# State and probability products of a linear-attention chunk as one piece over sixteen heads, with the query decayed in place

## What is computed

```python
def step(S, inp):
    qb, kb, vb = inp
    inter = jnp.einsum('bhcd,bhde->bhce', qb * decay_q[None, :, :, None], S)
    scores = jnp.einsum('bhcd,bhed->bhce', qb, kb) * dmask[None]
    intra = jnp.einsum('bhce,bhed->bhcd', scores, vb)
    S_new = lam_c[None, :, None, None] * S + jnp.einsum('bhcd,bhce->bhde', kb * decay_k[None, :, :, None], vb)
    return (S_new, inter + intra)
```

## Time and profile before

| | |
|---|---|
| median of three runs | 1953.87 us |
| the profiled execution | 1956.51 us |
| its span | 1954.7 us |
| TensorE busy | 1876.6 us (96%) |
| VectorE busy | 1084.2 us (55%) |
| ScalarE busy | 842.1 us (43%) |
| GpSimd busy | 438.3 us (22%) |
| mean granted clock of TensorE | 0.99 |
| block 0 (first q/k projection to that of block 1) | 17.05 to 122.84 us |
| end of attention (router product of block 7) | 1212.2 us |
| moved by DMA | 456.84 MB |

### The profile page before, as it was taken

How to read it: one execution, slowest core, us unless ns; L and a number is a source line. 1 busy time by engine, 2 the same in 40 slices (tenths; PEclk the granted TensorE clock), 3 DMA queues, 4 the chain that set the end, 5 groups by cost and what they waited for, 6 DMA issues and landing times.

```text
span 1954.7 us, 27560 instructions
## 1 busy us (share of the span) xinstructions
PE 1876.6 (96%) x9880; PEld 1529.3 (78%) x9880; DVE 1084.2 (55%) x2590; ACT 842.1 (43%) x1718; POOL 438.3 (22%) x438
## 2 busy tenths in 40 slices
PE   7789999999999998999999999999999999999997
PEld 5566777777777776777777778778999999999875
DVE  4556665454564563464454454353666667666566
ACT  4433443333343233334244233112666666666554
POOL 2301001001001000100100100120355666655322
PEclk9899999999999999999999999999999999999999
DMA  8988557656466447537647456687788989998597
GB/s 309 371 275 301 204 204 275 222 172 231 162 234 238 167 166 258 202 119 261 207 179 253 175 175 237 236 332 258 215 250 261 280 260 262 268 266 249 135 280 198
DMA packets 140869, 456.84 MB, mean 234 GB/s; under 512 B 17200, under 2 KB 17344, under 8 KB 123968
## 3 DMA queue, kind: packets, MB, share of 16 engines
q1 hardware_dynamic: 90720, 251.70, 36.7%
q0 software_dynamic: 49584, 203.33, 33.8%
q10 hardware_dynamic: 432, 0.07, 0.0%
HBM read 332.99 MB, written 122.04 MB: 233 GB/s over the span
## 4 chain that ended last, share of the span: by engine, by line
PE 88%; DVE 5%; DMA 3%; ACT 2%; issue 1%; another core or an unknown queue 0%; SPq 0%; POOL 0%; ACTq 0%; DVEq 0%
PE banks L797 24%; PE banks L799 24%; PE banks L798 24%; PE banks L866 5%; PE banks L880 2%; PE banks L886 2%; PE banks L992 2%; DMA att_w_lo<-att_w_split 1%; PE banks L873 1%; PE banks L830 1%; PE banks L998 1%; DMA out<-x 1%; PE banks L860 1%; DVE fin_stats L1538 0%; PE banks L908 0%
## 5 line engine op out<-in xcount | busy, mean ns | idle before, releaser
L797 PE MATMUL banks<-xT_hi,ffn_gate_up_hi_lo 128*128 128x512 f32 x704 | 288.5, 410 | 9.7 <-DMA xT_lo<-xt_scratch 3.2
L799 PE MATMUL banks<-xT_hi,ffn_gate_up_hi_lo 128*128 128x512 f32 x704 | 276.3, 392 | 0.0
L798 PE MATMUL banks<-xT_lo,ffn_gate_up_hi_lo 128*128 128x512 f32 x704 | 275.4, 391 | 0.0
L1070 ACT COPY q_one_head<-qT 32x128 f32<-32x128 f32 x512 | 150.9, 295 | 121.9 <-PE banks L866 116.8
L797 PE MATMUL banks<-moe_gu_hi,moe_xT_hi 128*128 128x352 f32 x568 | 189.4, 333 | 0.0
L799 PE MATMUL banks<-moe_gu_hi,moe_xT_lo 128*128 128x352 f32 x568 | 183.3, 323 | 0.0
L798 PE MATMUL banks<-moe_gu_lo,moe_xT_hi 128*128 128x352 f32 x568 | 182.6, 321 | 0.0
L797 PEld LDWEIGHTS banks<-xT_hi,ffn_gate_up_hi_lo 128*128 128x128 f32 x704 | 132.9, 189 | 44.3 <-issue 7.0
L683 POOL DMA_INDIRECT ffn_out<-moe_y,moe_x x71 | 124.9, 1760 | 155.4 <-ACT moe_gu_hi L1131 59.8
L798 PEld LDWEIGHTS banks<-xT_lo,ffn_gate_up_hi_lo 128*128 128x128 f32 x704 | 133.0, 189 | 29.2 <-issue 3.6
L799 PEld LDWEIGHTS banks<-xT_hi,ffn_gate_up_hi_lo 128*128 128x128 f32 x704 | 132.5, 188 | 28.8
(11 more groups left out here) (318 smaller groups left out, 4139.8 us busy)
## 6 DMA issues: line engine op xcount, KB each, us to landing
ffn_gate_up_hi_lo<-ffn_gate_up_split SPq DMA_DIRECT2D x66, 1024.0 KB
ffn_down_hi_lo<-ffn_down_split SPq DMA_DIRECT2D x66, 512.0 KB, 4.4
att_w_hi<-att_w_split SPq DMA_DIRECT2D x112, 256.0 KB, 5.3
att_w_lo<-att_w_split SPq DMA_DIRECT2D x112, 256.0 KB, 5.8
x_normed_by_expert<-x_normed POOLq DMA_DIRECT2D x26, 771.0 KB, 15.9
ffn_w_raw<-w_ffn SPq DMA_DIRECT2D x44, 384.0 KB, 6.0
ffn_gate_up_split<-ffn_gate_up_hi_lo SPq DMA_DIRECT2D x11, 1024.0 KB, 4.9
x_in<-x SPq DMA_DIRECT2D x32, 256.0 KB, 5.2
```

What stands on the lines that cost most here:

```text
L797: pe.matmul(out_ap, l_hi, r_hi, start=start, stop=False)
L798: pe.matmul(out_ap, l_hi, r_lo, start=False, stop=False)
L799: return pe.matmul(out_ap, l_lo, r_hi, start=False, stop=stop)
L1070: op = act.copy(qz[r, g % 2, j, :], qT[r, g, c * P:(c + 1) * P])
```

## The change

The two pieces become one, IP(c), with the state products of the four groups, then the probability products of all sixteen heads, in one bank of 512 columns. It waits for the last group's scores. `probs` has room for all four groups. ScalarE and VectorE evict the whole bank in one instruction each. The decayed q is written over q itself by a piece of its own, QD, on VectorE, which waits for ScalarE's four copies of the chunk (Z); the next block's q may be written only when the last chunk's IP is done on TensorE. All numbers of PLACES and OPENING are new. Waits for "the last weight" are now for the last of several in whichever order they stand.

```diff
+    "xin": (-31.52, -31.14, -18.03, -17.92,),
...
-    "wa": (5.53, 5.95, 9.34, 7.63, 9.92, 10.43, 10.08, 11.83, 11.97, 14.59, 17.75, 18.03, 22.85, 22.12, 24.74, 23.59,),
+    "wa": (3.51, 7.97, 8.26, 8.28, 8.94, 10.22, 10.68, 12.45, 13.8, 15.05, 16.73, 18.47, 23.22, 22.39, 22.92, 21.73,),
...
+    "QD": (21.59, 26.96, 34.86, 46,),
...
-    "ws": (3.07, 3.17, 7.17, 8.17, 10.88, 11.32, 13.32, 14.32, 15.32, 16.32, 17.32, 18.17, 23.02, 23.17, 23.32, 23.47,),
+    "ws": (16.22, 9.79, 17.24, 9.25, 19.16, 21.66, 28.21, 23.48, 32.67, 31.39, 31.98, 39.27, 40.36, 41.7, 40.49, 42.69,),
...
-    "IP": (22.6, 24.81, 28.65, 32.3, 37.22, 40.7, 46.32, 49.88,),
+    "IP": (24.98, 30.99, 40.28, 48.73,),
...
-PASSES = {"T1": 2, "QK": 12, "V": 12, "KT": 2, "S": 4, "IP": 6, "ST": 4, "OUT": 12, "T2": 2, "R1": 12, "R2": 2, "RK": 1,
+PASSES = {"T1": 2, "QK": 12, "V": 12, "KT": 2, "S": 4, "IP": 12, "ST": 4, "OUT": 12, "T2": 2, "R1": 12, "R2": 2, "RK": 1,
...
-        qd = sb("q_decayed", [G, P], scope=phase1)
-        probs = sb("probsT", [2, GH, P], scope=phase1)
+        probs = sb("probsT", [G, GH, P], scope=phase1)
...
             elif kind == "IP":
-                c, half = args
-                pe.wait_ge(v_piece, max(done("V", "S", a, c, 2 * half + 1), done("V", "V", a, c), done("V", "KT", a, c)))
-                for gl in range(2):
-                    g = 2 * half + gl
-                    pe.matmul(b[:, gl * P:(gl + 1) * P], state[:, g, :], qd[:, g, :], start=(gl == 0), stop=False,
+                c, = args
+                pe.wait_ge(v_piece, max(done("V", "S", a, c, G - 1), done("V", "V", a, c), done("V", "KT", a, c),
+                                        done("V", "QD", a, c)))
+                for g in range(G):
+                    pe.matmul(b[:, g * P:(g + 1) * P], state[:, g, :], qT[:, g, c * P:(c + 1) * P], start=(g == 0), stop=False,
                               skip_group_check=True)
-                for gl in range(2):
-                    g = 2 * half + gl
-                    cols = slice(gl * P, (gl + 1) * P)
+                for g in range(G):
+                    cols = slice(g * P, (g + 1) * P)
                     for j in range(GH):
                         r = slice(j * HD, (j + 1) * HD)
                         mm = pe.matmul(b[r, cols], v[:, c, g * P + j * HD:g * P + (j + 1) * HD],
-                                       probs[:, g % 2, j, :], start=False, stop=(gl == 1), skip_group_check=True)
+                                       probs[:, g, j, :], start=False, stop=(g == G - 1), skip_group_check=True)
...
                 if a and m == 0:
-                    act.wait_ge(p_piece, done("P", "S", a - 1, NC - 1, G - 1))
-                    act.wait_ge(v_piece, done("V", "KT", a - 1, NC - 1))
+                    act.wait_ge(p_piece, done("P", "IP", a - 1, NC - 1))
...
-                op = act.copy(oT_hi[:, 2 * half:2 * half + 2, :], chunked(b[:, 0:2 * P]))
+                op = act.copy(oT_hi[:, :, :], chunked(b))
...
-                ve.tensor_tensor(qd[:, :, :], qT[:, :, c * P:(c + 1) * P], dq[:, :, :], ALU.mult)
                 op = ve.tensor_tensor(kd[:, :], b, dk[:, :], ALU.mult)
+            elif kind == "QD":
+                c, = args
+                ve.wait_ge(a_piece, done("A", "Z", a, c, G - 1))
+                op = ve.tensor_tensor(qT[:, :, c * P:(c + 1) * P], qT[:, :, c * P:(c + 1) * P], dq[:, :, :], ALU.mult)
...
-                op = ve.tensor_tensor(oT_lo[:, gs, :], chunked(b[:, 0:2 * P]), oT_hi[:, gs, :].bitcast(F32),
-                                      ALU.subtract)
+                op = ve.tensor_tensor(oT_lo[:, :, :], chunked(b), oT_hi[:, :, :].bitcast(F32), ALU.subtract)
```

More of the change, by code:

```diff
@@ L99 @@
[L99 to L110, removed]
+    "xin": (-31.52, -31.14, -18.03, -17.92,),
+    "N1A": (-5.07,),
+    "N1B": (-1.92,),
+    "N1": (-1.67, 2.54, 2.87, 7.65,),
+    "T1": (4.49, 5.52, 7.6, 8.12,),
+    "wa": (3.51, 7.97, 8.26, 8.28, 8.94, 10.22, 10.68, 12.45, 13.8, 15.05, 16.73, 18.47, 23.22, 22.39, 22.92, 21.73,),
@@ new lines @@
+    "QK": (10.45, 10.56, 12.04, 13.66, 14.81, 14.95, 16.07, 16.43,),
+    "xr": (27.13, 32.3, 42.61, 48.08,),
+    "Z": (13.89, 15.32, 21.33, 22.5, 23.65, 23.78, 27.64, 27.9, 29.13, 29.3, 33.27, 35.14, 38.73, 42.29, 42.93, 45.06,),
+    "QD": (21.59, 26.96, 34.86, 46,),
+    "KT": (19.21, 29.28, 34.61, 46.53,),
+    "S": (17.98, 20.2, 22.22, 22.51, 25.87, 26.54, 27.95, 29.25, 32.56, 33.09, 37.34, 37.62, 43.02, 43.07, 47.64, 47.81,),
+    "V": (21.44, 22.15, 24.45, 25.52,),
+    "IP": (24.98, 30.99, 40.28, 48.73,),
@@ new lines @@
+    "ST": (27.59, 31.41, 40.69, 50.1,),
+    "OUT": (30.11, 35.5, 45.63, 50.81,),
+    "LO": (36.01, 50.91,),
+    "LN": (38.12, 53.23,),
+    "L": (38.72, 53.49,),
+    "LX": (40.86, 54.54,),
+    "x1o": (42.87, 45.14, 55.25, 60.01,),
+    "T2": (42.02, 45.02, 57.18, 57.65,),
+    "xto": (59.66,),
+    "R1": (58.72,),
+    "R2": (59.18,),
+    "SM1": (59.68,),
+    "SM2": (59.95,),
+    "SM3": (60.82,),
+    "SM4": (63.91,),
+    "CM": (61.51,),
+    "RK": (64.56,),
+    "sc": (64.43,),
+    "PG": (66.52,),
@@ L755, in sp_piece @@
                 if u < RAW:
-                    sp.wait_ge(v_piece, done("V", "W", 0, NW - 1))
+                    sp.wait_ge(v_piece, max(done("V", "W", 0, u) for u in range(NW)))
                 else:
@@ L850, in pe_attention @@
                     else:
-                        pe.wait_ge(v_piece, done("V", "W", a, 11))
+                        pe.wait_ge(v_piece, max(done("V", "W", a, 8 + k) for k in range(KT)))
                 for k in range(KT):
@@ L893, in pe_attention @@
                     else:
-                        pe.wait_ge(v_piece, done("V", "W", a, 15))
-                pe.wait_ge(v_piece, done("V", "IP", a, c, 1))
+                        pe.wait_ge(v_piece, max(done("V", "W", a, 12 + k) for k in range(KT)))
+                pe.wait_ge(v_piece, done("V", "IP", a, c))
                 for k in range(KT):
@@ L1071, in act_attention @@
             elif kind == "IP":
-                c, half = args
-                if half == 0 and c > 0:
-                    act.wait_ge(p_piece, done("P", "OUT", a, c - 1))
-                elif half == 0 and a:
-                    act.wait_ge(p_piece, done("P", "OUT", a - 1, NC - 1))
-                op = act.copy(oT_hi[:, 2 * half:2 * half + 2, :], chunked(b[:, 0:2 * P]))
+                c, = args
+                if c or a:
+                    act.wait_ge(p_piece, done("P", "OUT", *divmod(NC * a + c - 1, NC)))
+                op = act.copy(oT_hi[:, :, :], chunked(b))
             elif kind == "R1":
```

32 lines of the change are left out of this document (6 added, 26 removed), and 19 rows, old and new, of the table OPENING.

## The result

The changed kernel takes 1938.15 us (median of 4 runs, 1936.11 to 1940.40) against 1954.69 for the kernel before (1952.63 to 1955.94): ratio 0.9919, interval 0.9906 to 0.9931, so it is faster by 16.5 us. The forecast was 1939. The profiled execution took 1936.11 us, the fastest of its four, where that of the kernel before, 1956.51, lies above its whole range; so the spans, 1954.7 and 1934.3, differ by 20.4 us.

The account below looks back on a forecast made before the run. TensorE, busy 1876.6 of 1954.7 us, was taken as the bound. -9.0 + 6 - 6 - 6 = -15 us on 1956.5 gave 1941.5; the median lying 2.6 lower, the forecast was 1939 us, range 1924 to 1952.

Parts of the forecast that it names:

- Part 1: TensorE's merged piece: one step into and out of the 32-column form saved, 28 x 0.32 us behind block 0, -9.0 us.
- Part 2: Longer merged evictions and q's decay in place, on ScalarE and VectorE: covered by products of 2.8 us, cost nothing.
- Part 3: End of block 0: a split weight's store joins the transfer chain, block 1 starts at 128.6 against 122.84, +6 us.
- Part 4: Block 5: the late sixth q/k weight now goes ahead of the seventh, -6 us, ends -1.4 and -8.4.
- Part 5: TensorE's other waits behind block 0, such as k's transposes and the half product's scores: -6 us, ends -10 and +5.
- the charge of +3 for the projection of chunk 2: New wait: this projection needs the second score's bank right behind it, some 0.45 us in seven blocks, +3.
- A: Rival: block 0's chain gets no longer, TensorE let go at 120 or earlier; 1928 us, chance 0.15.
- D: Rival: no change, only the steps saved and a chain of +9 in block 0; 1953 us, chance 0.08.
- B: Rival: only the form steps are saved, the waits of parts 4 and 5 move elsewhere; 1948 us, chance 0.17.
- C: Rival: steps belong to each group of column tiles, so nothing of part 1 comes; near 1948 us, chance 0.05.
- E: Rival: slower, block 0's last split weight's store lands late, block 1 starts near 142 us; 1961 us, chance 0.09.

Follow-up runs that it names:

- second pair: Both kernels profiled again, on chips of different levels: the changed kernel 1942.39 us (0.9887), the kernel before 1955.16 us (one run).
- halves: The changed kernel with the merged piece's products issued in two runs, key groups 0 and 1, then 2 and 3: 1950.23 us, 0.9926.
- quarters: The changed kernel with the merged piece's products issued in four runs, one key group at a time: 1968.76 us, 1.0024.

## Why the prediction was right

The median came out 1 us from the forecast, and that is closer than the parts. The sum was -15 us on the profiled execution; that fell by 20.4, and the medians by 16.5. In the first pair of profiles block 1 starts 5.8 us later, and all behind it takes 26.2 us less, where parts 1, 4 and 5 have 21. In the second pair, of different chips, it starts 2.7 later and all behind takes 16.5 less.

**Part 1, the merged piece, -9.0.** Right, in size and in cause. The step costs 0.32 to 0.33 in the traces and 0.24 to 0.32 in the times. Taken from the undisturbed blocks 4 and 6 of both kernels (147.8 and 148.3 against 146.0 to 146.3) the gain is 1.7 to 2.2 us a block, where four steps make 1.3. The rest is no wait, for TensorE waits less than 0.1 us in block 4 and 0.3 in block 6 of that profile of before; it was not taken apart.

**Part 2, evictions and q, 0.** Nearly right for the new order, and only there. In the changed kernel only the waits for the cast count, 4.4 us in the first profile and 4.9 in the second. In the old order the same piece makes TensorE wait 30 us, where the earlier trace rows has 7.6 for the same causes, more than its steps save. "The order has one state update and then a gate, up or down product of 2.8 us behind it in nearly all chunks" was the sentence that carried this, and with the old order it would not have held for k's transpose. So the redrawn places are no addition to the merging but its condition: on two chips of one level, merging in the old places is +18 us by the medians, merging with the new places -21.

**Part 3, block 0, +6.** The number was right (128.66 against 128.6), by errors that cancel: the third x load is issued at 117.8 and not at 113.5, the store takes 5.06 and not 7.0, the load 3.62 and not 6.0. The step that failed is "TensorE itself is ready before, as it was before the change". It was ready at 118.5 (122.84 less 4.34 of waiting) and is at 125.3 (128.66 less 3.4): its waits in block 0 grew from 18.3 to 22.7 us, 7.9 of them ahead of the first x1 transpose, and half clock from 10.2 to 20.5, half of it from 96.0 on. The prediction also read the whole 4.34 us as room, where VectorE's low part of x left 1.2. By that part alone block 1 would start at 127.5, 5.9 us later than before, so the added store accounts for about 1 us of the delay and not for 6. This is why taking the store or the residual store out of the chain gave 1 to 3 us, not 6. Nor is +6 the change's price everywhere: on one chip the kernel before with the two weights exchanged, which leaves block 0 as it was, starts block 1 at 126.7, and the changed one at 129.4, so +2.7.

**Part 4, block 5, -6.** About right. The first pair of profiles has -7.9, the second, of different chips, -6.0 (160.9 and 154.9), of which 1.3 are part 1, and the exchange alone made -4.9 in the time. On one chip, with only the exchange, block 5 is 1.0 us longer than in the changed kernel, no more than its steps. But the wait did not go: it is 1.5 to 5.5 us in the eight traces with the new places, with half clock behind it in all but the first.

**Part 5, the other waits, -6.** Too large. TensorE's waits from the start of block 1 to the router's product of block 7, without those of the two late weights of parts 3 and 4, are 14.5 us in the first profile of before and 10.6 in that of after, so -3.9; in the second pair they are 9.4 and 10.2, no gain at all. k's transposes (-6.0) and the half product's scores (-1.6) went, and the charge of +3 for the projection of chunk 2 hardly came: what stands ahead of it are two waits of 0.2 us. New were the 4.4 us for the cast, which I had not seen, because no row of before has ScalarE's queue blocked by the shared expert's eviction ahead of a half product. And the 6.0 are a wait that the second profile of before does not have. The first pair gained more behind block 0 than the parts add up to: blocks 1, 2, 4 and 6 are 2.8 to 3.2 us shorter each, of which four steps make 1.3 and the waits only a part.

**The rivals.** A and D are out by their starts of block 1 (120 or earlier, a chain of +9). B's condition, waits of parts 4 and 5 that move elsewhere, came in part, in blocks 3 and 5: in the first pair not for half the sum, in the second, where part 5 gave nothing, for about half. C is refuted by halves and quarters. E had no store that lands late. D's price does not follow from its own terms: B with a chain of +9 is -3, 1951 and not 1953, which changes nothing here.

## What to carry to other kernels

A change of TensorE's column form has a price per change, here a third of a microsecond there and back, so group instructions by form before counting instructions. A merged piece also merges its eviction: look for the piece that takes the same bank next, and move that with it, or the merging costs more than it saves. Where a transfer ends a stretch, ask what would end it next, for the distance to that is all that shortening the transfer can give: here TensorE stood idle for 3.4 us, but VectorE's part was ready only 1.2 ahead of the late weight.

## What the runs showed of the hardware

ScalarE's cast of a finished bank was held until GpSimd's indirect scatters had ended, though ScalarE was idle: it started 2.0 to 3.4 us after the start of the last product in six of seven blocks with the merged piece in the old places, 0.8 to 2.6 in the first profile of the kernel before, and 0.34 where nothing holds it. Five of the six begin 1.0 to 1.1 us after the end of the last of four scatters, the one of block 1 during the fourth. With the scatter made to wait for the cast the hold was gone in all blocks, which shows that it hangs on the scatter. By what path is open, and so is why the second profile of the kernel before has casts that become ready during scatters and start after 0.34 us. All traces with the hold, but the first of before, come from the two chips where the kernel before takes 1963 us.
